# Second mixture of experts: rows gathered by a table of tokens in place of rows scattered to their places

## The reference, cut to what matters

```
logits = flat_x @ Wg + bg                       # 2048 tokens, 4 experts
top_vals, top_idx = top_k(logits, 2)
probs = softmax over the two chosen
for i in range(4):
    score = where(token chose i, probs[:, i], -inf)
    sel_p, sel_idx = top_k(score, capacity = 512)
    tok = flat_x[sel_idx]
    y = (gelu(tok @ W1[i]) @ W2[i]) * p
    out = out.at[sel_idx].add(y)
x = layernorm(x + out)
```

## Time and profile before

| | |
|---|---|
| runs of the kernel before | 4956.53, 4962.67, 4965.86 us |
| profiled execution: span from first to last instruction | 4953.7 us |
| mean granted TensorE clock | 0.894 of full |
| PE busy | 3940.3 us (80%) |
| DVE busy | 2817.3 us (57%) |
| ACT busy | 1646.4 us (33%) |
| POOL busy | 1437.1 us (29%) |

### The profile page before, as it was taken

How to read it: one execution, slowest core, us unless ns; L and a number is a source line. 1 busy time by engine, 2 the same in 40 slices (tenths; PEclk the granted TensorE clock), 3 DMA queues, 4 the chain that set the end, 5 groups by cost and what they waited for, 6 DMA issues and landing times. The chain is left out here.

```text
span 4953.7 us, 62201 instructions
## 1 busy us (share of the span) xinstructions
PE 3940.3 (80%) x19774; PEld 3051.4 (62%) x19774; DVE 2817.3 (57%) x4906; ACT 1646.4 (33%) x3379; POOL 1437.1 (29%) x1236
## 2 busy tenths in 40 slices
PE   7885999989999697753995994787878688828993
PEld 7885777767777475542553883555656476606772
DVE  5554444453444476871224874999999755523335
ACT  4343222232222120020222674555555422203431
POOL 0001101110000005663113542999999600020002
PEclk9998999999999798956997997999899899958996
DMA  3324566653333452144996546222222211033324
GB/s 112 122 85 152 117 132 123 131 128 86 83 102 87 129 167 69 40 166 151 334 318 211 182 135 226 77 85 81 81 81 89 80 53 63 30 110 123 105 96 121
DMA packets 557200, 602.49 MB, mean 122 GB/s; under 512 B 166070, under 2 KB 439543, under 8 KB 551425
## 3 DMA queue, kind: packets, MB, share of 16 engines
q1 hardware_dynamic: 508720, 491.05, 32.0%
q0 software_dynamic: 43520, 101.18, 8.2%
q10 hardware_dynamic: 4816, 8.53, 0.5%
HBM read 444.17 MB, written 198.34 MB: 130 GB/s over the span
## 5 line engine op out<-in xcount | busy, mean ns | idle before, releaser
L2274 PE MATMUL d_py<-d_h,d_ident 128*128 128x256 f32 x2048 | 529.6, 416 | 169.9 <-POOL d_h L2104 151.9
L2112 POOL TENSOR_TENSOR d_dBu<-d_B,d_dtu 128x1024 f32<-128x1024 f32 x256 | 597.1, 2364 | 117.9 <-DMA d_dt<-dt 117.9
L2274 PEld LDWEIGHTS d_py<-d_h,d_ident 128*128 128x128 f32 x2048 | 418.0, 208 | 277.8 <-POOL d_h L2104 180.0
L722 PE MATMUL a_pB<-a_uhi,a_whi 128*128 128x512 f32 x1152 | 495.1, 430 | 49.4 <-DVE a_ulo L609 43.5
L722 PE MATMUL a_pB<-a_uhi,a_wlo 128*128 128x512 f32 x1152 | 464.6, 403 | 0.0
L722 PE MATMUL a_pB<-a_ulo,a_whi 128*128 128x512 f32 x1152 | 463.8, 403 | 0.0
L2158 ACT ACTIVATE d_ph<-d_dt,d_A 128x255 f32<-128x255 f32 x1024 | 425.8, 461 | 0.2
L2218 DVE TENSOR_TENSOR_SCAN d_ph<-d_ph,d_dBu 128x1024 f32<-128x1024 f32 x160 | 366.0, 2287 | 24.4 <-ACT d_ph L2158 12.1
L1054 POOL TENSOR_TENSOR b_kv<-b_c 128x128 f32 (+11 forms) x256 | 100.3, 432 | 801.9 <-DMA b_c<-ctx_turned 797.3
L722 PEld LDWEIGHTS a_pB<-a_uhi,a_whi 128*128 128x128 f32 x1152 | 225.0, 195 | 117.6 <-DVE a_wlo L613 36.5
L695 DVE SCALAR_TENSOR_TENSOR a_W<-a_pG,a_cB,a_M 128x256 f32<-128x256 f32 (+1 forms) x384 | 142.7, 413 | 217.5 <-PE a_pG L743 193.7
(11 more groups left out here) (461 smaller groups left out, 9459.7 us busy)
## 6 DMA issues: line engine op xcount, KB each, us to landing
c_gu<-w_gu SPq DMA_DIRECT2D x64, 768.0 KB, 8.3
a_wraw<-w_bc SPq DMA_DIRECT2D x48, 768.0 KB, 7.4
a_alall<-alpha SPq DMA_DIRECT2D x24, 1024.0 KB, 5.0
slots<-a_idz POOLq DMA_DIRECT2D x64, 256.0 KB, 4.6
c_wd<-w_down SPq DMA_DIRECT2D x64, 256.0 KB, 7.8
c_xb<-slots SPq DMA_DIRECT2D x64, 256.0 KB, 9.2
slots_y<-c_y POOLq DMA_DIRECT2D x64, 256.0 KB, 6.9
f_w1r<-w SPq DMA_DIRECT2D x64, 256.0 KB, 2.7
```

The costliest lines, as they stand in the source:

```text
L722: ins = nc.tensor.matmul(out, a[:, k, cols], b[:, k, ts], start=(k == 0 and n == 0), stop=(k == F - 1 and n == 2))
L2112: pool.tensor_tensor(dBu[c % RB][:, :, :], B_sb[i][:, q * G:(q + 1) * G, :], dtu_sb[i][:, f, :].unsqueeze(1).to_broadcast([P, G, L]), ALU. ...
L2274: ins = nc.tensor.matmul(py[f % 2][:, 0:L], ident_sb[:, :], h_sb[c % RH][:, n, :], start=False, stop=(q == Q - 1 and n == G - 1))
```

## The change

No row is scattered any more. `moe1_route` makes instead a table `row_token` in the on-chip memory, with 128 lanes and 16 columns (4 experts of 4 blocks of 128 rows): entry (lane, block) is the number of the token whose row stands there. It is built so: DVE splits the rank into a part `part` (which block of 128 in the expert) and a `lane`; `named` holds, for each token and choice, 16 columns with the token's number in the column of its block and zeros elsewhere; `at_lane` holds 128 columns with a one at its lane. The product of `at_lane` and `named`, summed over 16 tiles and two choices (32 products of 128x128 by 128x16, in full float32), is the table. `at_lane` of the first 11 tiles is made by DVE, that of the last 5 by POOL (`ON_POOL`).

`moe1_experts` then fetches a block of 128 rows by an indirect DMA from the token-ordered activations `x5_tok`, with a semaphore for each block, so that PE waits block by block. POOL's loop over experts is written out. `xt` is not loaded, `rows` is gone and is not zeroed in phase a. One table is new (`tokens_of`) and one is wider (`ramp`). The table lives in a space `f0` around both phases, whose closing adds a barrier.

```diff
@@ moe1_route, SP
-            for dst, src in ((before_sb[:, :], before), (ramp_sb[:, :], ramp[0:EX].partition_broadcast(P)),
+            for dst, src in ((before_sb[:, :], before), (ramp_sb[:, :], ramp.partition_broadcast(P)), (tok_sb[:, :], tokens_of),
...
-            sp.dma_start(xt[:, :, :], x_tok.rearrange("(c p) n -> p c n", p=P)).then_inc(s_xt, 16)
             sp.wait_ge(s_pl, 2)
@@ moe1_route, POOL
-            pool.wait_ge(s_xt, 16)
-            pool.wait_ge(s_pl, 2)
-            for c in range(TILES):
+            pool.wait_ge(s_const, 16 * CONSTS)
+            pool.wait_ge(s_lane, 1)
+            for c in range(TILES - ON_POOL, TILES):
                 for k in range(TOP):
-                    pool.indirect_dma_start(x_rows, bass.IndirectOffsetOnAxis(ap=pl[:, c, k:k + 1], axis=0), xt[:, c, :], None,
-                                            bounds_check=EX * SEL - 1, oob_is_err=False).then_inc(s_scat, 16)
-            pool.wait_ge(s_scat, TILES * TOP * 16)
+                    ins = pool.tensor_scalar(at_lane[:, c, k, :], ramp_sb[:, :], lane[:, c, k:k + 1], None, ALU.is_equal)
+                ins.then_inc(s_at_pool, 1)
@@ moe1_route, DVE, between rk and ok
+            link(nc.vector.tensor_tensor(past ..., ALU.is_ge))
+            link(nc.vector.tensor_reduce(part ..., AX.X, ALU.add))
+            nc.vector.scalar_tensor_tensor(lane[:, :, :], part[:, :, :], -float(P), rk[:, :, :], ALU.mult, ALU.add).then_inc(s_lane, 1)
+            link(nc.vector.scalar_tensor_tensor(block_of[:, :, :], idf[:, :, :], float(RT), part[:, :, :], ALU.mult, ALU.add))
+            link(nc.vector.tensor_tensor(blocks, ramp_sb ..., block_of ..., ALU.is_equal))
+            nc.vector.tensor_tensor(named ..., tok_sb ..., ALU.mult).then_inc(s_named, 1)
+            dve.wait_ge(s_lane, 1)
+            for c in range(TILES - ON_POOL):
+                nc.vector.tensor_tensor(at_lane[:, c, :, :], ramp_sb ..., lane ..., ALU.is_equal).then_inc(s_at, 1)
@@ moe1_route, DVE, last
             nc.vector.tensor_tensor(wk[:, :, :], pr[:, :, :], ok[:, :, :], ALU.mult).then_inc(s_pl, 1)
+            dve.wait_ge(s_tab, 1)
+            nc.vector.tensor_copy(row_token[:, :], pR[0][:, 0:EX * RT]).then_inc(s_pl, 1)
@@ moe1_route, PE, last
+            pe.wait_ge(s_named, 1)
+            for c in range(TILES):
+                if c < TILES - ON_POOL:
+                    pe.wait_ge(s_at, c + 1)
+                else:
+                    pe.wait_ge(s_at_pool, c - (TILES - ON_POOL) + 1)
+                for k in range(TOP):
+                    ins = nc.tensor.matmul(pR[0][:, 0:EX * RT], at_lane[:, c, k, :], named[:, c, k, :],
+                                           start=(c == 0 and k == 0), stop=(c == TILES - 1 and k == TOP - 1))
+            ins.then_inc(s_tab, 1)
@@ moe1_experts, POOL
-                pool.dma_start(x_sb[i][:, :, :], x_rows[bass.ds(e * SEL, SEL), :].rearrange("(c p) n -> p c n", p=P)).then_inc(s_x[i], 16)
+                for c in range(RT):
+                    n = e * RT + c
+                    pool.indirect_dma_start(x_sb[i][:, c, :], None, x_tok, bass.IndirectOffsetOnAxis(ap=row_token[:, n:n + 1], axis=0),
+                                            bounds_check=T - 1, oob_is_err=False).then_inc(s_x[i][c], 16)
@@ moe1_experts, PE
-                    pe.wait_ge(s_x[i], r * 16 + 16)
                     for c in range(RT):
+                        pe.wait_ge(s_x[i][c], r * 16 + 16)
@@ decoder
-              ..., (slots, rows))
+              ..., (slots,))
```

More of the change, by code:

```diff
@@ L2592, with moe1_route @@
 FAR = 1 << 20
-def moe1_route(nc, x_tok, x_feat, w_router, b_router, before, ramp, ident, digits, digits_int, x_rows, places, weights):
+def moe1_route(nc, x_feat, w_router, b_router, before, ramp, tokens_of, ident, digits, digits_int, row_token, places, weights):
     ROUNDS, TRIALS = 10, 7
     QT = BANK
+    RT = SEL // P
+    ON_POOL = 5
     QUARTERS = T // QT
@@ L2627, in moe1_route @@
         wk = m.sb("wk", [P, TILES, TOP])
+        edge, past = m.sb("edge", [P, RT - 1]), m.sb("past", [P, TILES, TOP, RT - 1])
+        part, lane, block_of = (m.sb(n, [P, TILES, TOP]) for n in ("part", "lane", "blockof"))
+        at_lane = m.sb("atlane", [P, TILES, TOP, P])
+        named = m.sb("named", [P, TILES, TOP, EX * RT])
         pR = [m.ps(f"pR{i}") for i in range(QUARTERS)]
@@ L2631, in moe1_route @@
         s_raw, s_rows = m.sem("raw"), m.sem("rows")
[L2632 to L2633 removed]
+        s_lane, s_at, s_at_pool, s_named, s_tab = (m.sem(n) for n in "lane at at_pool named tab".split())
+        s_const, s_lv, s_loop, s_log, s_d, s_e, s_count, s_total, s_taken, s_before, s_pl, s_out = (
+            m.sem(n) for n in "const lv loop log d e count total taken before pl out".split())
         block = phase.enter_context(nc.Block())
[L2635 removed]
+        CONSTS = 8
         @block.sync
         def _(sp):
[L2639 removed]
+            for dst, src in ((before_sb[:, :], before), (ramp_sb[:, :], ramp.partition_broadcast(P)), (tok_sb[:, :], tokens_of),
                              (rw[:, :, :], w_router.rearrange("(k p) e -> p k e", p=P)), (rb[:, :], b_router.partition_broadcast(P)),
@@ L2677, in _ @@
             link(nc.vector.memset(floor[:, :], 0))
+            for n in range(RT - 1):
+                link(nc.vector.memset(edge[:, n:n + 1], float((n + 1) * P)))
             dve.wait_ge(s_const, 16 * CONSTS)
@@ L2747, in _, with flat @@
             link(nc.vector.tensor_reduce(rk[:, :, :].rearrange("p c k -> p (c k)"), wt[:, :, :, :].rearrange("p c k e -> p (c k) e"), AX.X, ALU.add))
+            def flat(v):
+                return v.rearrange("p c k -> p (c k)")
+            pairs = TILES * TOP
+            link(nc.vector.tensor_tensor(past[:, :, :, :].rearrange("p c k j -> p (c k) j"), flat(rk[:, :, :]).unsqueeze(2).to_broadcast([P, pairs, RT - 1]),
+                                         edge[:, :].unsqueeze(1).to_broadcast([P, pairs, RT - 1]), ALU.is_ge))
+            link(nc.vector.tensor_reduce(flat(part[:, :, :]), past[:, :, :, :].rearrange("p c k j -> p (c k) j"), AX.X, ALU.add))
+            nc.vector.scalar_tensor_tensor(lane[:, :, :], part[:, :, :], -float(P), rk[:, :, :], ALU.mult, ALU.add).then_inc(s_lane, 1)
+            link(nc.vector.scalar_tensor_tensor(block_of[:, :, :], idf[:, :, :], float(RT), part[:, :, :], ALU.mult, ALU.add))
+            blocks = named[:, :, :, :].rearrange("p c k q -> p (c k) q")
+            link(nc.vector.tensor_tensor(blocks, ramp_sb[:, 0:EX * RT].unsqueeze(1).to_broadcast([P, pairs, EX * RT]),
+                                         flat(block_of[:, :, :]).unsqueeze(2).to_broadcast([P, pairs, EX * RT]), ALU.is_equal))
+            nc.vector.tensor_tensor(named[:, :, :, :].rearrange("p c k q -> p c (k q)"), named[:, :, :, :].rearrange("p c k q -> p c (k q)"),
+                                    tok_sb[:, :].unsqueeze(2).to_broadcast([P, TILES, TOP * EX * RT]), ALU.mult).then_inc(s_named, 1)
+            dve.wait_ge(s_lane, 1)
+            for c in range(TILES - ON_POOL):
+                nc.vector.tensor_tensor(at_lane[:, c, :, :], ramp_sb[:, :].unsqueeze(1).to_broadcast([P, TOP, P]),
+                                        lane[:, c, :].unsqueeze(2).to_broadcast([P, TOP, P]), ALU.is_equal).then_inc(s_at, 1)
             link(nc.vector.tensor_scalar(ok[:, :, :], rk[:, :, :], float(SEL), None, ALU.is_lt))
@@ L2830, in outputs @@
                 pool.dma_start(y_rows[bass.ds(e * SEL, SEL), :].rearrange("(c p) n -> p c n", p=P), y_sb[:, :, :]).then_inc(s_out, 16)
[L2831 to L2836, removed]
+            for e in range(EX):
+                outputs(e)
+                if e + 2 < EX:
+                    rows(e + 2, e % 2)
             pool.wait_ge(s_out, EX * 16)
```

24 lines of the change are left out of this document (13 added, 11 removed).

## The result

Four runs of the changed kernel lie between 4925.34 and 4935.62 us, median 4931.13, beside 4961.18 for the kernel before: ratio 0.9933, 95% interval 0.9919 to 0.9947. That is 30 us less, against 23.3 forecast; the forecast's 4939.4 is 8.3 above the median. The profiled execution has a span of 4923.7 us, 30.0 under that of before.

What follows compares the result with a forecast made beforehand. It took POOL's list of 32 scatters to bound the kernel for 46 us. Terms +0.5, -22.3, -2.0 and +0.5 sum to -23.3 us, from 4962.7 to 4939.4, range 4929 to 4949.

Steps and rivals of the forecast that it cites:

- slow rival: Two: table products end the routing, 4942.5 us, chance 0.15; gathers starve beside weights in the experts' opening, 4969.7, chance 0.02.
- the zeroing: Dropping the zeroing of rows in phase a: 0 us, ends -1 and +1 for the second half's loads.
- the collision: Routing: POOL's ten compares and DVE's two-input compares exclude each other, adding 3.5 us to DVE's list, ends 0 and 4.5.
- its rival: No collision: POOL's and DVE's compares do not hinder each other; 3.5 us less, 4935.9 us, chance 0.22.
- DVE's list: New DVE instructions behind the rank in the routing: 5.9 us, by which pl and wk come later.
- stores, issue to SP's branch: SP's stores of places and weights at the routing's end: 13.9 us, ends 10.9 and 13.9.
- products: PE's 32 table products in the routing: 13.8 us, ending with handover and copy 5.2 us before the stores land.
- routing's part, together: SP's first DMA of the experts comes at 4441.8 instead of 4464.15: -22.3 us.
- opening of the experts: SP's first DMA to PE's first product, with four gathers for expert 0: -2.0 us, ends -3.3 and +1.
- end of the experts: The extra barrier closing the experts' phase: +0.5 us, ends 0 and +1.
- The sign that the forecast named for being wrong here: For the zeroing: PE's stretches in phase a showing other than 46.65 us busy of 48.
- The base: The starting time for the sum: the runs' median 4962.7 us, 9.0 above the profiled span of 4953.7.

Runs made afterwards that it cites:

- e1: The changed kernel run again in five rounds with no edit: median 4933.14 us, ratio 0.9942 to the kernel before.
- e5: The changed kernel with all 16 tiles' lane compares on DVE and none on POOL: median 4936.61 us, ratio 0.9944 to the kernel before.
- e6: The changed kernel with all 32 lane compares on POOL and none on DVE: median 4932.4 us, ratio 0.9934 to the kernel before.
- e3: The kernel before with POOL's 32 scatters and their wait left out, experts working on zero rows: median 4933.06 us, ratio 0.994.
- e7: The changed kernel with SP waiting for the fourth block of expert 0's rows before its first weights: ratio 0.9942 to the kernel before.

## Why the prediction was right or wrong

The path was right: the stores set the end of the routing, with the products 3.3 us ahead of them (forecast 5.2), and neither slow rival came. Two steps on the way were wrong: the zeroing, which the forecast had at 0, and the collision, where its rival was nearer. That the median fell by 30 and not 23.3 us comes mostly from the first.

| term | forecast | measured |
|---|---|---|
| opening of the routing | +0.5 | +0.3 (from SP's first DMA to the reduce 73.3 us before, 73.6 now; 74.05 in e1) |
| DVE's list | +5.9 | +5.9 |
| collision with POOL | +3.5 | +0.6 |
| stores, issue to SP's branch | 13.9 | 12.7 |
| products | 13.8 | 13.8 |
| boundary | 1.0 | 0.9 |
| routing's part, together | -22.3 | -26.6 |
| opening of the experts | -2.0 | +0.6 |
| end of the experts | +0.5 | +1.4 |
| zeroing | 0 | -6.6, error 1.3 |
| outside the span | 0 | -1.2 |

Without the last two rows the sum is -24.3, 1.0 from the forecast, because errors of both signs cancel. With them it is -32, against the runs' 30; the error of the zeroing and the wander of the medians cover the difference. That the forecast came so near is in part luck.

The step that failed is "The zeroing: ... so 0, ends -1 and +1": measured were -6.6 us. It was judged from one pair of stretches with the same 46.65 us of PE. Two windows of 48 us can't show 6 us spread over 4340, or in phases that hold no zeroing at all; the ends were meant for the loads of `u_raw` alone. The sign that the forecast named for being wrong here was blind as well: the changed kernel has 46.64 us of PE in both stretches, but 268 and 267 instructions in them at a granted clock of 1.00, where there were 258 and 258 at 0.96. The busy share does not tell the pace. Nor does the clock of these stretches explain the gain: over the 18 profiles it lies between 0.93 and 1.00, at 1.00 in some with the zeroing and at 0.96 in some without. Why the zeroing's absence is worth 6.6 us stays open.

The collision: the earlier trace rows showed a DVE instruction of 0.16 us stretched to 2.33 beside a POOL operation. The forecast took this for nearly full alternation, in which "POOL's 4.0 us are added to DVE's list". e5 and e6 show the reverse here: POOL pays. DVE's 17 instructions took 6.5 us and not 9 to 10, and no compare was far over 0.42. The POOL operation of the earlier trace rows had two inputs in memory and was six times as long; whether that makes the difference no run tests. The Trainium skill, page "SBUF — State Buffer", section "SBUF: two separate sides", says that who starts first holds the pair "for the whole instruction" and that "the other fully blocks" (the forecast's "the loser" stands under "Terms" of that page). The runs agree that the two hinder each other, and disagree on the rest: POOL's compare of 1.1 us spans three DVE compares, of which only one is longer, by 0.09 us. The forecast gave the end without a collision (4935.9) a chance of 0.22; that was the nearer.

The stores: the ends of 10.9 and 13.9 held, but the slow row was taken, which had scatters beside it (13.9 and 14.3 in the two profiles with them). Without them it was 12.1 to 13.3 over 16 profiles, 12.9 in e3.

The opening: the forecast named the load of the DMA engines and allowed 1.3 us for it in the landing of the fourth block; measured were 11.7 instead of 9.1. The row of the landings came from a phase without a stream of weights, and e7 shows that this is nearly the whole difference.

The end: the forecast had the barrier (0.3) and not the drain, though the earlier trace rows showed a drain of 2.67 us behind indirect DMAs, and the experts' phase now has 16 of them.

The base: the forecast added its sum to the median, 9.0 above the profiled span. Of that only 2.8 lay outside the span; the rest was that this execution was the fastest of its three. That was harmless for a difference, but it let 1.2 us outside the span go unseen.

## What to carry to other kernels

Taking a queue of DMAs off one engine's list pays down to what stands behind it: here 32 scatters, one every 1.29 us, whose stretch was 46 us long, were worth 33 alone (e3) and 26.6 with the table's work in their place, since the stores behind them took 12.7 to 12.9. Once these are issued first, and the products take one pass, 6.4 more are won in the distance A. A gather beside a stream of weights wants the stream held back until the rows are in. A term priced at nothing on the word of one window needs bounds as wide as the wander of the whole run, and an interleaved pair of kernels to settle it.

## What the runs showed of the hardware

- Beside DVE compares with two inputs in on-chip memory, a POOL compare of 128x128 took 1.02 to 1.12 us instead of 0.60, and DVE's took 0.50 instead of 0.41 one time in three.
- The same 32 products of 16 columns took 13.80 us as f32 (64 passes, one every 0.22 us) and 7.1 in one pass as fp32r, the last ones paced by POOL's compares.
- POOL's drain at a phase's end took 34 ns in e3's routing, where POOL issued nothing, 713 at the end of the experts with four plain loads, 1695 there with 16 gathers, and 2671 behind the 32 scatters of the routing.
- The first eight gathers of 128 rows landed in 3.8 us in the median with the stream of weights held back, and in 6.1 with it beside them.
- From the rank to the first product the changed kernel's clock was at 0.50, the 1.2 GHz level, though PE worked 13.8 us at the table; before, with PE idle behind the rank, it was 0.50 to 4464 and 0.57 in the opening.
